# A new step table for the products of a two-layer adaptive-norm and expert kernel: linear products further ahead, copies a step earlier, two operand buffers in turn

## The chip, the cores and the metric

The kernel runs on one core of a Trainium2 chip. The metric is the device time of one execution in microseconds (us), here the median of three runs. The core has five engines that run their own instruction queues and meet only at semaphores: TensorE (PE) multiplies matrices, VectorE (DVE) and ScalarE (ACT) work elementwise, GpSimd (POOL) does one clip and all indirect DMAs, and SyncE (SP) issues most loads and stores. A matmul leaves its result in PSUM, and DVE or ACT must read it before the bank is used again.

## The reference

The input `x` is (4, 1024, 1024). Layer 0 adds a linear product of a gate over a two-way decaying scan; layer 1 adds a mixture of 32 experts (four per token) and a shared network. Cut to what matters:

```
nf, nb = scan(ekv, decay), scan(ekv, decay, reverse=True)       # along time, per channel
df, db = scan(ek, decay),  scan(ek, decay, reverse=True)
out  = sigmoid(r) * (nf + nb - ekv + euk*v) / max(df + db - ek + euk, 1e-8) * (0.8 + 0.2*tf)
x    = x + (out0 @ (weight * scale_weight[:, None]).T + bias)   # r = x, k = v = fside
x    = x + ffn(out1)                                            # out1: same scan, second w and u
ffn(x): h = rmsnorm(x, norm_w); top-4 of softmax(h @ router_w.T)
        routed = sum of topk_w * (silu(h@w1[:, :I]) * (h@w1[:, I:])) @ w2
        shared = (silu(h@sg) * (h@su)) @ sd
        return x + routed + shared
```

All products are made in parts: an operand is split into a high part and a remainder (`hi`, `lo`), and each product is three matmuls for each 128 x 128 block: hi*hi, hi*lo, lo*hi.

## The kernel before

Time runs in three stages.

**Units alone.** The scans are 32 *units*, one for each batch and each 128 channels, on tiles of 128 x 1024. A unit has two passes (`l` = 0 and 1, for the two layers). DVE carries it: four scans and about eight other passes over the tile. ACT supplies exponentials and the inverse, POOL the clip of `k` at 30 (`clip`, L509). The operand of a unit is loaded in two DMAs: `side_t` into the buffer `K`, `x_t` into `X`. There is one `K`, so `load_side(u + 1)` waits until unit u has made its last read of it, in the second pass (`wv_done`, L886). The chain then is the DMA, `clip`, ACT's `side_exp` (L573) and DVE's first operation of the next unit (L867). The first 8 units run with only the splitting of the shared weights beside them.

**Halves.** The tokens are cut into 8 halves of 512. A half is 32 *steps*; a step is one product of 24 matmuls of 512 columns on PE. Steps 0 to 15 mix the linear products of this half (`step_l(o)`, L) with the down products of the half before (`step_d(o)`, D): L0 L1 D0 L2 D1 ... L7 D6 D7. Behind every L product DVE adds it to x (L1192, `XL`, two slots), ACT makes the second gate's sigmoid, DVE multiplies with the ratio (L1185, `C1`) and ACT squares that (L691); PE sums the squares into `SUM_BANK` in `square_sums` (L1339). Behind a D product DVE adds the residual (L1148), PE turns it to token order (`out_by_token`, L1365), ACT copies it to `RS` (`out_copy`, L674) and SP stores it; a copy waits for the store before it. After step 15 comes the *normalization*: DVE and ACT make 1/sqrt of the mean (L1153 to L1161), and PE, DVE and ACT pass the eight normalized tiles through `by_token` (L1349, L1351). Steps 16 to 31 are gate and up products: ACT makes silu, DVE the product (`gated_up`, L1118 and L1124), ACT the high part (L669) and DVE the remainder (L1129). In the last eight of them the next half's operand `C` is loaded (`load_cl`, SP), its high part copied (ACT L726) and its remainder taken (DVE L1139), at the same step.

A product's result lies in one of four PSUM banks, so the product of a step waits until the result of four steps before has been read. Its weights come in two DMAs of 512 KB that SP issues three products ahead.

The units 8 to 31 run inside halves 0 to 5, four in each. The function `fill(h, i, ...)` holds what an engine does at step i, and `unit` calls it at eight fixed places of a unit, so the order of unit work and step work is fixed by the code. Halves 6 and 7 have no units. In half 0 there are no D products.

**Experts.** The routed tokens are 149 tiles of 128 tokens. `step(g, j)` on PE makes four quarter products with the first weights, the transposes of the former tile's activations (L1454) and of the next tile's tokens (L1398), and the second product of the former tile (L1479).

Of the kernel before, what the change touches and what calls it, by code (L numbers as in the profile page):

```python
# [44 lines left out]
def step_d(o):  # L45
    return 2 * o + 2 if o < CB - 1 else 2 * CB - 1
# [10 lines left out]
def adaln_moe(nc, x_t, side_t, cond, w_all, u_all, lin_sb, norm_w, router_t, shared_w, expert_w, out):  # L57
# [12 lines left out]
    with ctx:  # L70
# [85 lines left out]
        lsb_neg = sb("lsb_neg", CB)  # L156

# [30 lines left out]
        xl_sem = [sem(f"xl_in{i}") for i in range(2)]  # L188
# [81 lines left out]
        def with_halves(eng, unit, fill, tail, alone, weights=lambda: None):  # L270


            with eng.Fori(0, 2 * UNITS_PER_HALF - 1) as u:
                unit(u, lambda i: alone(u, i))
            last = 2 * UNITS_PER_HALF - 1

# [6 lines left out]
            unit(last, last_alone)  # L283
            for q in range(UNITS_PER_HALF):
                unit(2 * UNITS_PER_HALF + q, lambda i: fill(0, q * FILLS_PER_UNIT + i, first=True, prev=False, next_=True))
            with eng.Fori(1, HALVES - 2) as h:
                for q in range(UNITS_PER_HALF):
                    unit(h * UNITS_PER_HALF + (2 * UNITS_PER_HALF + q),
# [8 lines left out]
        def _(sp):  # L297
# [47 lines left out]
            def load_xl(h, o):  # L345
                rows, cols = half_rows(h, o)
                wait(sp, "res", h * CB + (o - 1))
                sp.dma_start(XL[o % 2], x_t[rows, cols]).then_inc(xl_sem[o % 2], 16)

            def fill(h, i, first, prev, next_):  # L350
# [3 lines left out]
                if not before_all(h):  # L354
                    for o in range(CB):
                        if i == step_l(o):
                            load_xl(h, o)
                        if i == step_l(o):
                            load_rl(h, o)
                        if prev and i == step_d(o) + 4:  # L360
# [5 lines left out]
                if next_:  # L366
                    for c in range(CB):
                        if i == STEPS - CB + max(c - 1, 0):
# [16 lines left out]
            def unit(u, fill):  # L385
# [25 lines left out]
            def alone(u, i):  # L411

                if isinstance(u, int):
                    return
# [33 lines left out]
        def _(pool):  # L448
# [4 lines left out]
            pool.wait_ge(s["masks"], 4)  # L453
# [6 lines left out]
            pool.wait_ge(s["masks"], 7)  # L460
# [43 lines left out]
            def clip(u):  # L504
# [4 lines left out]
                pool.tensor_scalar(EK, K, 30.0, None, ALU.min).then_inc(s["kc"], 1)  # L509

            clip(0)
            with pool.Fori(1, BLOCKS + 1) as u:
                clip(u)
# [39 lines left out]
        def _(sc):  # L553
# [21 lines left out]
            def load_side(u):  # L575
                wait(sc, "wv_done", 2 * u)
# [982 lines left out]
```

## Time and profile before

| what | value |
|---|---|
| median of three runs | 4997.55 us (4991.03 to 4998.45) |
| the profiled execution, its own time | 4997.07 us |
| its span, first to last instruction | 4995.4 us |
| PE busy | 4492.5 us (90%) |
| DVE busy | 2646.0 us (53%) |
| ACT busy | 1729.7 us (35%) |
| granted TensorE clock, mean | 0.949 of full speed |

The shares are means over three stages with different limits: up to 353 us PE has little to do, to 2298 us PE and DVE share the work, and from there PE is all but full. They have to be read by stage.

### The profile page before, as it was taken

Reading aid. Unit: us, or ns where it says so; the run is one execution under the profiler, and the core shown is the slowest. Engines: PE = TensorE matmul, PEld = TensorE weight load, DVE = VectorE, ACT = ScalarE, POOL = GpSimd, SP = SyncE. Lnnn points to the kernel's source line nnn. Section 1 sums busy time; section 2 is a strip of 40 time slices with the busy share of each in tenths; the row PEclk is TensorE's granted clock in tenths of the full one; section 3 lists DMA queues with packets and bytes.
Section 4 is the critical chain, followed back from the end, with each engine's and each line's share of the span. In section 5 each row is a group of like instructions: output and inputs, shape, how many; then the busy total and the mean of one; then the engine's idle time right before and its main releaser. Section 6 shows DMA issues by size and latency. Waiting matters only on the chain.

```text
span 4995.4 us, 62260 instructions
## 1 busy us (share of the span) xinstructions
PE 4492.5 (90%) x19732; PEld 3555.7 (71%) x19735; DVE 2646.0 (53%) x2844; ACT 1729.7 (35%) x2532; POOL 698.0 (14%) x933
## 2 busy tenths in 40 slices
PE   4446888888888899999999999999999999999998
PEld 1124666666666677877888888788788887888787
DVE  8988878787878774443323343343443235233332
ACT  4444444444444433223223232333432124222331
POOL 1000000000000000541111111111111111111111
PEclk7777999999999999999999999999999999999999
DMA  5564656665656566866435454555654246354442
GB/s 207 206 223 152 222 203 219 206 215 204 218 206 216 201 228 212 238 190 234 109 66 153 110 160 110 156 160 160 210 160 109 59 109 206 78 140 109 142 123 59
DMA packets 247943, 835.17 MB, mean 167 GB/s; under 512 B 28160, under 2 KB 61056, under 8 KB 222976
## 3 DMA queue, kind: packets, MB, share of 16 engines
q1 hardware_dynamic: 172944, 572.77, 32.8%
q0 software_dynamic: 47728, 160.07, 15.0%
q10 hardware_dynamic: 27136, 100.67, 5.4%
q8 instruction: 68, 1.11, 0.1%
q14 instruction: 67, 0.55, 0.0%
HBM read 652.40 MB, written 181.01 MB: 167 GB/s over the span
## 4 chain that ended last, share of the span: by engine, by line
PE 66%; DVE 14%; issue 8%; ACT 6%; DMA 4%; POOL 1%; DVEq 0%; ACTq 0%; SPq 0%; POOLq 0%
PE ps L1465 33%; PE ps L1479 16%; PE ps L1329 10%; PE ps L1398 3%; DMA work<-side_t 2%; DVE work L876 2%; DVE work L873 2%; DVE work L879 1%; POOL work L509 1%; PE ps L1454 1%; DVE work L883 1%; DVE work L886 1%; ACT work L567 1%; ACT work L565 1%; DVE work L900 1%
## 5 line engine op out<-in xcount | busy, mean ns | idle before, releaser
L1465 PE MATMUL ps<-halves 128*128 128x512 f32 x7152 | 1744.3, 396 | 25.4 <-DVE halves L1240 21.8
L1329 PE MATMUL ps<-halves 128*128 128x512 f32 x6144 | 1500.5, 405 | 110.1 <-DVE work L1118 69.5
L1465 PEld LDWEIGHTS ps<-halves 128*128 128x128 f32 x7152 | 1327.7, 189 | 299.2 <-DVE halves L1240 24.0
L1329 PEld LDWEIGHTS ps<-halves 128*128 128x128 f32 x6144 | 1192.0, 195 | 409.1 <-issue 122.4
L1479 PE MATMUL ps<-halves 128*128 128x512 f32 x3576 | 834.9, 389 | 1.3 <-DVE halves L1260 1.3
L1479 PEld LDWEIGHTS ps<-halves 128*128 128x128 f32 x3576 | 671.2, 188 | 140.7 <-DVE halves L1260 1.6
L1244 DVE TENSOR_TENSOR halves<-ps,halves 128x1024 fp32r<-128x1024 f32 x150 | 183.7, 1225 | 927.2 <-ACT halves L757 927.2
L1240 DVE TENSOR_TENSOR halves<-work,halves 128x1024 fp32r<-128x1024 f32 (+1 forms) x320 | 440.5, 1435 | 111.9 <-ACT halves L761 111.9
L757 ACT ACTIVATE halves<-ps 128x1024 fp32r<-128x1024 f32 x150 | 153.8, 1025 | 887.1 <-PE ps L1465 887.1
L761 ACT ACTIVATE halves<-work 128x1024 fp32r<-128x1024 f32 (+1 forms) x320 | 369.7, 1221 | 97.2 <-PE ps L1479 66.5
L509 POOL TENSOR_SCALAR work<-work 128x1024 f32<-128x1024 f32 x33 | 98.0, 2969 | 1728.3 <-DMA work<-side_t 1728.3
L1266 DVE TENSOR_SCALAR work<-ps,acc 128x512 f32<-128x512 f32 x149 | 111.6, 749 | 273.3 <-PE ps L1479 266.6
L1309 PE MATMUL ps<-plain,ident 128*128 128x512 f32 x128 | 88.5, 780 | 184.9 <-ACT halves L641 184.9
L490 POOL DMA_INDIRECT out<-work,add_idx x149 | 236.2, 1585 | 131.0 <-POOL add_idx L487 125.3
L487 POOL COPY add_idx<-acc 128x1 int32 x149 | 27.0, 181 | 1610.2 <-DVE work L1266 1610.2
L1256 DVE TENSOR_TENSOR work<-ps,work 128x256 f32<-128x256 f32 x298 | 124.9, 419 | 231.9 <-ACT work L785 224.1
L795 ACT ACTIVATE work<-ps,acc 128x512 f32<-128x512 f32 x149 | 101.5, 681 | 395.7 <-PE ps L1479 388.5
L1260 DVE TENSOR_TENSOR halves<-ps,halves 128x256 fp32r<-128x256 f32 x298 | 112.2, 419 | 218.6 <-ACT halves L789 218.6
L785 ACT ACTIVATE work<-ps 128x256 f32<-128x256 f32 x298 | 113.3, 380 | 306.0 <-PE ps L1465 305.9
L1309 PEld LDWEIGHTS ps<-plain,ident 128*128 128x128 f32 x128 | 30.0, 250 | 229.0 <-ACT halves L641 197.0
L480 POOL DMA_INDIRECT work<-rows_dram,row_idx x151 | 152.5, 1010 | 129.0 <-POOL row_idx L476 122.8
L789 ACT ACTIVATE halves<-ps 128x256 fp32r<-128x256 f32 x298 | 97.6, 379 | 197.7 <-PE ps L1454 197.7
(179 smaller groups left out, 3893.4 us busy)
## 6 DMA issues: line engine op xcount, KB each, us to landing
halves<-split_dram SPq DMA_DIRECT2D x512, 512.0 KB, 5.1
work<-expert_w SPq DMA_DIRECT2D x192, 1024.0 KB, 5.3
split_dram<-halves ACTq DMA_DIRECT2D x32, 1024.0 KB, 6.0
plain<-shared_w SPq DMA_DIRECT2D x32, 512.0 KB, 4.1
gated_dram<-work ACTq DMA_DIRECT2D x32, 512.0 KB, 3.2
work<-x_t ACTq DMA_DIRECT2D x32, 512.0 KB, 5.2
work<-side_t ACTq DMA_DIRECT2D x32, 512.0 KB, 5.3
ratio_dram<-work ACTq DMA_DIRECT2D x32, 512.0 KB, 3.6
```

The lines of the kernel that those rows point to most:

```text
L480: pool.indirect_dma_start(hx, None, rows_dram[:, :], bass.IndirectOffsetOnAxis(row_idx[:, :].bitcast(u32), 0)).then_inc(s["rows_in"], 16)
L490: pool.indirect_dma_start(out[:, :], bass.IndirectOffsetOnAxis(add_idx[:, :].bitcast(u32), 0), y, None, compute_op=ALU.add).then_inc(s["y_ ...
L509: pool.tensor_scalar(EK, K, 30.0, None, ALU.min).then_inc(s["kc"], 1)
L757: sc.activation(xhi, ps_xt[:, :], ACT.Copy).then_inc(s["x_hi"], 1)
L761: sc.activation(whi[q][:, part], staged(q, part), ACT.Copy).then_inc(s["w_hi"], 1)
L1240: ve.tensor_tensor(wlo[q][:, part], staged(q, part), whi[q][:, part].bitcast(f32), ALU.subtract).then_inc(s["w_lo"], 1)
L1244: ve.tensor_tensor(xlo, ps_xt[:, :], xhi.bitcast(f32), ALU.subtract).then_inc(s["x_lo"], 1)
L1256: ve.tensor_tensor(part, ps_h[:, a * 512 + 256:a * 512 + 512], part, ALU.mult).then_inc(s["act_done"], 1)
L1329: last = pe.matmul(bank(k % 4), w, op[:, part], start=(c == 0 and w is w_hi and op is hi), stop=(c == CB - 1 and w is w_lo))
L1398: last = pe.transpose(ps_xt[:, c * P:(c + 1) * P], hx[:, c * P:(c + 1) * P], ident[:, :])
L1465: last = pe.matmul(ps_h[:, a * 512:a * 512 + 512], xp[:, xk * P:(xk + 1) * P], wp[:, rhs], start=(xk == 0 and xp is xhi and wp is whi[q]), ...
L1479: last = pe.matmul(ps_y[:, h * 512:h * 512 + 512], ap_[:, (q * 2 + k) * P:(q * 2 + k + 1) * P], wp[:, rhs:rhs + 512], start=(q == 0 and k ...
```

## The change

The formulas for the steps become tables. The down products move back, the linear ones forward: L at 0, 1, 2, 4, 6, 8, 10, 11 and D at 3, 5, 7, 9, 12, 13, 14, 15. `XL` has four slots (two of them are the tiles `Z0` and `Z1`, free at that time). The last sum of squares comes after step 14, not 15, and ACT takes the logarithm straight from `SUM_BANK` at step 15 (`R_AT`), ahead of the DVE's own mean; DVE makes `root` and the first two normalized tiles before the last D product's sum. The turns and copies of the outputs have steps of their own. The high part of `C` is copied at steps 23 to 30, its remainder taken at 24 to 31, and its loads are issued from step 22 on.

The two operand buffers are used in turn: in an even unit `side_t` lies in `K` and `x_t` in `X`, in an odd one the other way round. So the next unit's `side_t` is loaded when the first pass has been gated, and `x_t` in the second pass. ACT's `side_exp` moves before the second inverse. In the expert stage PE makes two quarter products before the transposes of the activations, not one.

```diff
+STEP_L = (0, 1, 2, 4, 6, 8, 10, 11)
+STEP_D = (3, 5, 7, 9, 12, 13, 14, 15)
+TURN_AT = (5, 7, 9, 11, 13, 14, 15, 17)
+COPY_AT = (6, 8, 10, 12, 14, 15, 17, 18)
+SQUARE_AT = (3, 4, 5, 7, 9, 11, 13, 13)
+SUM_AT = (5, 5, 6, 8, 10, 12, 13, 14)
+R_AT = 2 * CB - 1
-    return 0 if o == 0 else 2 * o - 1
-    return step_l(o) + 3 if o < CB - 1 else 2 * CB - 1
-    return 2 * o + 2 if o < CB - 1 else 2 * CB - 1
+C_LOAD = (22, 22, 23, 24, 25, 26, 27, 29)
+C_HIGH = (23, 24, 25, 26, 27, 28, 29, 30)
+C_LOW = (24, 25, 26, 27, 28, 29, 30, 31)
...
+        side_of, x_of = (K, X), (X, K)
-        XL, RL, Z, T = [XL0, XL1], [RL0, RL1], [Z0, Z1], SQ
+        XL, RL, Z, T = [Z0, Z1, XL0, XL1], [RL0, RL1], [Z0, Z1], SQ
...
-                        if i == step_l(o):
+                        if i == (step_d(o - 4) + 1 if o >= 4 else o // 2):
                             load_xl(h, o)
-                        if i == step_l(o):
+                        if i == (step_l(o - 2) + 2 if o >= 2 else o):
                             load_rl(h, o)
...
-            def load_side(u):
-                wait(sc, "wv_done", 2 * u)
-                sc.dma_start(K, side_t[ds(u % BLOCKS * P, P), :]).then_inc(s["k_in"], 16)
+            def load_side(u, par):
                 sc.wait_ge(s["gated"], u + 1)
-                sc.dma_start(X, x_t[ds(u % BLOCKS * P, P), :]).then_inc(s["x_in"], 16)
+                sc.dma_start(side_of[par], side_t[ds(u % BLOCKS * P, P), :]).then_inc(s["k_in"], 16)
...
                 fill(5)
+                side_exp(u + 1)
                 fill(6)
                 inverse(1)
                 fill(7)
-                side_exp(u + 1)
...
-                    if i == 2 * CB:
-                        sc.wait_ge(s["mean"], h + 1)
-                        sc.activation(R, SQ, ACT.Ln).then_inc(s["r_ln"], 1)
+                    if i == R_AT:
+                        sc.wait_ge(s["sums"], h * CB + CB)
+                        sc.activation(R, SUM_BANK, ACT.Ln, bias=eps[:, :], scale=1.0 / CH).then_inc(s["r_ln"], 1)
...
+                    if i == 2 * CB:
+                        root(h)
+                        normalize(h, 0)
+                        normalize(h, 1)
...
                 first_product(j, 0)
+                first_product(j, 1)
                 transpose_act(g - 1, 0)
                 transpose_act(g - 1, 1)
-                first_product(j, 1)
                 transpose_x(g + 1)
```

The order on three queues. First PE at the end of the L and D products, in the loop over halves 1 to 5. L1329 (after: L1380) is a product, L1365 (L1416) a turned output, L1339 (L1390) a sum of squares, L1349 and L1351 (L1400, L1402) the first normalized tile. Before:

```order
L1329 MATMUL ps<-halves 128x512 x48
L1362 REGISTER_ALU
L1365 MATMUL ps<-ident,work 128x128 x4
L1339 MATMUL ps<-work,ones 128x512
L200 REGISTER_ALU
L1329 MATMUL ps<-halves 128x512 x24
L1362 REGISTER_ALU
L1365 MATMUL ps<-ident,work 128x128 x4
L1339 MATMUL ps<-work,ones 128x512
L1349 MATMUL ps<-ident,work 128x128 x4
L1351 MATMUL ps<-work,rw 32x512
```

After:

```order
L235 REGISTER_ALU
L1380 MATMUL ps<-halves 128x512 x24
L1413 REGISTER_ALU
L1416 MATMUL ps<-ident,work 128x128 x4
L1390 MATMUL ps<-work,ones 128x512
L235 REGISTER_ALU
L1380 MATMUL ps<-halves 128x512 x24
L1413 REGISTER_ALU
L1416 MATMUL ps<-ident,work 128x128 x4
L1400 MATMUL ps<-ident,work 128x128 x4
L1402 MATMUL ps<-work,rw 32x512
```

The last sum of squares now has a product and a turned output between itself and the first normalized tile; before it stood directly in front of it.

Second, ACT where the third unit of such a half ends and the fourth begins. L726 (after: L771) copies a high part of `C`, L669 (L713) one of the activations, L573 is `side_exp`, L591 (L635) begins the next unit, and the DMA of the ratio closes a unit. Before:

```order
L573 ACTIVATE work<-work 128x1024
L636 DMA ratio_dram<-work 128x1024
L666 REGISTER_ALU
L669 ACTIVATE halves<-work 128x512
L721 ISA
L723 REGISTER_ALU
L726 ACTIVATE halves<-work 128x512
L589 REGISTER_ALU
L591 ISA
L591 ACTIVATE edge_in<-work,edge 128x1
```

After:

```order
L611 ACTIVATE work<-work 128x512
L766 ISA
L768 REGISTER_ALU
L771 ACTIVATE halves<-work 128x512
L680 DMA ratio_dram<-work 128x1024
L710 REGISTER_ALU
L713 ACTIVATE halves<-work 128x512
L771 ACTIVATE halves<-work 128x512
L633 REGISTER_ALU
L635 ISA
L635 ACTIVATE edge_in<-work,edge 128x1
```

Two copies of `C` now stand before the fourth unit's first work where one stood, and `side_exp` has gone from this place.

Third, PE in a tile of the expert stage. L1465 (after: L1516) is a quarter product of 12 matmuls, L1454 (L1505) the transposes of the activations, L1398 (L1449) those of the tokens. Before:

```order
L1465 MATMUL ps<-halves 128x512 x12
L1450 ISA
L200 ISA
L1454 MATMUL ps<-ident,work 128x128 x2
L1450 REGISTER_ALU
L200 REGISTER_ALU
L1454 MATMUL ps<-ident,work 128x128 x2
L1465 MATMUL ps<-halves 128x512 x12
L1395 REGISTER_ALU
L1398 MATMUL ps<-ident,work 128x128 x8
L1465 MATMUL ps<-halves 128x512 x24
```

After:

```order
L1516 MATMUL ps<-halves 128x512 x24
L1501 ISA
L235 ISA
L1505 MATMUL ps<-ident,work 128x128 x2
L1501 REGISTER_ALU
L235 REGISTER_ALU
L1505 MATMUL ps<-ident,work 128x128 x2
L1446 REGISTER_ALU
L1449 MATMUL ps<-ident,work 128x128 x8
L1516 MATMUL ps<-halves 128x512 x24
```

The matmuls are the same; the two groups of transposes have become one.

## Rows read from the trace of the kernel before

**Rows 1.** Busy time by stretch: us, then PE, PEld, DVE, ACT, POOL, PEclk, DMA share, GB/s.

```profile
459.84:1699.84 1240.00, 1059.73 (x4337) 810.16 (x4337) 1006.39 (x906) 525.78 (x774) 59.52 (x20) 0.93 0.61 212
1449.04:1466.09 17.05, 15.41 (x49) 5.18 (x49) 11.55 (x17) 9.01 (x16) 0.00 (x0) 0.83 0.00 1
1466.09:1573.67 107.58, 92.40 (x394) 75.57 (x393) 83.00 (x70) 41.23 (x61) 3.45 (x1) 0.94 0.64 223
1573.67:1699.84 126.17, 105.22 (x429) 81.82 (x429) 106.88 (x97) 54.98 (x79) 8.30 (x3) 0.92 0.67 227
1699.84:1931.21 231.37, 209.15 (x868) 161.70 (x868) 154.97 (x166) 83.47 (x128) 6.21 (x3) 0.94 0.62 214
1824.71:1931.21 106.50, 100.41 (x428) 79.64 (x428) 60.48 (x81) 33.23 (x51) 3.40 (x2) 0.96 0.69 239
```

**Rows 2.** What PE waited for, 1449.04:1699.84: us in total, times, longest.

```profile
PE ps L1349 <- DVE work L1169: 19.7, 2, 10.1
PE ps L1329 <- DVE work L1118: 12.2, 3, 6.8
PE ps L1339 <- ACT work L691: 5.7, 2, 4.2
PE ps L1329 <- DVE halves L1129: 4.1, 1, 4.1
PE ps L1365 <- ACT work L674: 3.7, 1, 3.7
```

**Rows 3.** What DVE waited for in the same period.

```profile
DVE halves L1139 <- ACT halves L726: 14.5, 8, 4.3
DVE work L1124 <- PE ps L1329: 4.7, 1, 4.7
DVE halves L1129 <- ACT halves L669: 3.9, 1, 3.9
DVE work L898 <- issue: 3.5, 5, 1.1
DVE work L867 <- ACT work L573: 2.9, 1, 2.9
DVE work L1157 <- ACT work L701: 2.9, 1, 2.9
DVE work L898 <- ACT work L614: 1.4, 1, 1.4
```

**Rows 4.** What DVE waited for in the stretch 0:459.84.

```profile
DVE work L867 <- ACT work L573: 15.2, 8, 2.8
DVE plain L1185 <- ACT work L569: 4.3, 4, 1.1
```

**Rows 5.** Timeline, PE in half 6 and ACT in half 4: start, us, line, count.

```profile
2004.05 54.73 PE L1329 MATMUL ps<-halves 128*128 128x512 f32 x240
...
1488.24 0.60 ACT L674 ACTIVATE work<-ps 128x512 f32<-128x512 f32 x1 [10.99 <-DMA out<-work]
```

**Rows 6.** Landing of SP's weight loads, 1466:1600: count, KB, median us.

```profile
halves<-split_dram SPq DMA_DIRECT2D x38, 512.0 KB, 4.6
```

**Rows 7.** Timeline of POOL and DVE where a clip runs beside DVE.

```profile
1575.53 0.69 DVE L1139 TENSOR_TENSOR halves<-work,halves 128x512 fp32r<-128x512 f32 x1 [1.22 <-ACT halves L726]
...
1579.45 2.77 POOL L509 TENSOR_SCALAR work<-work 128x1024 f32<-128x1024 f32 x1 [59.21 <-DMA work<-side_t]
1579.99 1.05 DVE L1139 TENSOR_TENSOR halves<-work,halves 128x512 fp32r<-128x512 f32 x1 [2.03 <-ACT halves L726]
```

**Rows 8.** Timeline of PE in one tile of the expert stage.

```profile
3008.36 2.89 PE L1465 MATMUL ps<-halves 128*128 128x512 f32 x12
3011.09 0.60 PE L1454 MATMUL ps<-ident,work 128*128 128x128 f32 x4
3011.44 3.02 PE L1465 MATMUL ps<-halves 128*128 128x512 f32 x12
3014.30 1.04 PE L1398 MATMUL ps<-ident,work 128*128 128x128 f32 x8
```

More of the change, by code:

```diff
@@ L187, in adaln_moe @@
         put_sem = [sem(f"put_out{i}") for i in range(PUTS)]
-        xl_sem = [sem(f"xl_in{i}") for i in range(2)]
+        xl_sem = [sem(f"xl_in{i}") for i in range(4)]
         w_in = [sem(f"w_in{q}") for q in range(GROUPS)]
@@ L270, in with_halves @@
         def with_halves(eng, unit, fill, tail, alone, weights=lambda: None):
-            with eng.Fori(0, 2 * UNITS_PER_HALF - 1) as u:
-                unit(u, lambda i: alone(u, i))
+            with eng.Fori(0, UNITS_PER_HALF - 1) as v:
+                for par in range(2):
+                    unit(2 * v + par, par, lambda i: alone(2 * v + par, i))
             last = 2 * UNITS_PER_HALF - 1
+            unit(last - 1, 0, lambda i: alone(last - 1, i))
             def last_alone(i):
@@ L281, in last_alone @@
                     weights()
-            unit(last, last_alone)
+            unit(last, 1, last_alone)
             for q in range(UNITS_PER_HALF):
-                unit(2 * UNITS_PER_HALF + q, lambda i: fill(0, q * FILLS_PER_UNIT + i, first=True, prev=False, next_=True))
+                unit(2 * UNITS_PER_HALF + q, q % 2, lambda i: fill(0, q * FILLS_PER_UNIT + i, first=True, prev=False, next_=True))
             with eng.Fori(1, HALVES - 2) as h:
                 for q in range(UNITS_PER_HALF):
-                    unit(h * UNITS_PER_HALF + (2 * UNITS_PER_HALF + q),
+                    unit(h * UNITS_PER_HALF + (2 * UNITS_PER_HALF + q), q % 2,
                          lambda i: fill(h, q * FILLS_PER_UNIT + i, first=False, prev=True, next_=True))
@@ L346, in load_xl @@
                 rows, cols = half_rows(h, o)
-                wait(sp, "res", h * CB + (o - 1))
-                sp.dma_start(XL[o % 2], x_t[rows, cols]).then_inc(xl_sem[o % 2], 16)
+                if o < 2:
+                    wait(sp, "l_tr", h)
+                else:
+                    wait(sp, "res", h * CB + (o - 3))
+                sp.dma_start(XL[o % 4], x_t[rows, cols]).then_inc(xl_sem[o % 4], 16)
             def fill(h, i, first, prev, next_):
@@ L383, in store_out, with unit @@
                 sp.dma_start(to, RS.rearrange("p (t c) -> p t c", c=P)).then_inc(s["o_out"], 16)
-            def unit(u, fill):
+            def unit(u, par, fill):
                 for i in range(FILLS_PER_UNIT):
@@ L508, in clip @@
                 apart(pool)
[L509 to L513, printed above, removed]
+                pool.tensor_scalar(EK, side_of[par], 30.0, None, ALU.min).then_inc(s["kc"], 1)
+            clip(0, 0)
+            with pool.Fori(0, BLOCKS // 2) as v:
+                clip(2 * v + 1, 1)
+                clip(2 * v + 2, 0)
             pool.wait_ge(s["zero_set"], 1)
@@ L1199, in fill @@
                             ve.wait_ge(s["c1"], h * CB + (o + 1))
-                            ve.scalar_tensor_tensor(RES[:, part], XL[o % 2], lsb[:, CB + o:CB + o + 1], C1[o],
+                            ve.scalar_tensor_tensor(RES[:, part], XL[o % 4], lsb[:, CB + o:CB + o + 1], C1[o],
                                                     ALU.add, ALU.add).then_inc(s["res"], 1)
                     if i == 2 * CB:
-                        normalize(h)
+                        for o in range(2, CB):
+                            normalize(h, o)
+                        split_z_lo(h, CB - 1)
                     if i == 2 * CB + 2:
@@ L1411, in half @@
                     for o in range(CB):
-                        if i == square_step(o):
+                        if i == sum_step(o):
                             square_sums(h, o)
-                        if not first and i == step_d(o) + (2 if o < CB - 2 else 1):
+                        if not first and i == turn_step(o):
                             out_by_token(h - 1, o)
```

95 lines of the change are left out of this document (56 added, 39 removed).

## The prediction, made before the changed kernel ran

> **What bounds the kernel now.** I read the time by stretch first [rows 1]. A *period* goes from one half's first normalized tile to the next half's. Five periods with units in them, from 459.84 to 1699.84, take 1240.0 us, so 248.0 each. In one of them the normalized tiles take 17.05 us, the sixteen gate and up products 107.58, and the sixteen L and D products with the normalization behind them 126.17. Neither engine is full: over the five periods PE is busy 1059.7 us of 1240.0 and DVE 1006.4. The two wait for each other through the four banks.
>
> Then I read who waits. PE [rows 2] waits for the first normalized tile (19.7 us in two places, 10.1 in the larger), for DVE to free a bank (12.2), for a square (5.7), for the remainder of the activations that D0 reads (4.1), and for an output copy (3.7). DVE [rows 3] waits 14.5 us for the high parts of C, because ACT makes them in the same step, 4.7 for a late up product, 3.9 for a high part that stands on ACT behind an output copy, 2.9 for `side_exp` and 2.9 for the root.
>
> DVE is the engine to count with. It has 83.00 us of work in the gate stage and 106.88 in the L and D stage [rows 1]. PE's own time is less: ten products take 54.7 us in half 6, where nothing holds them [rows 5], so sixteen take 88; and a whole L and D stage without units takes 106.5, of which PE is busy 100.4 and idle 6.1, nearly all of it before the first normalized tile [rows 1].
>
> **The gate stage (108 us, six times).** The tables take three waits of DVE away or shorten them. The high part of C comes a step before its remainder, so the 11 to 14.5 us go: I count 11 here and the rest in the L and D stage, since two of the eight stand behind the stage's end. The 4.7 us for the up product went with PE's 3.7 us wait for the output copy, which moves behind the next product. Of the 3.9 us on the high part some 3.5 stays: ACT waits for the store of output 6 before it copies output 7 (10.99 us idle before that copy [rows 5]), and the store is still issued at step 18. The 1.4 and one 1.1 of L898 stay (ACT's inverse stands behind that copy), and about 1.1 us of short gaps between the two operations of `gated_up`. So DVE needs 83.0 + 3.5 + 1.5 + 1.1 + 1.1 = 90.2 us, against a PE floor of 88. Set beside each other step by step (5.5 us a product on PE; on DVE, per fill, 6.7 us for three scans, 5.5 for the next four operations, 1.2 and 3.9 or 5.1 for the rest), the bank for step 30 is free at 75 and wanted at 78, and the one for the next half's step 0 is free at 90.2 and wanted at 89.5. Both waits for banks (12.2 us) shrink to under 1. **The stage goes from 107.6 to 90.2.**
>
> **The L and D stage (126 us, five times with units).** D0 now follows three L products, so the 4.1 us wait for the remainder goes. The linear result has two steps until its gate is multiplied in all places but two, so most of the short waits on L1185 and L898 go; `side_exp` is early (2.9). The root: ACT's logarithm starts at the last sum, which comes one product (5.5 us) sooner. DVE's wait of 2.9 goes, and 1.3 us of DVE work (the last residual) moves behind the first normalized tile, where DVE waits anyway. So DVE needs 106.9 - 1.3 + 2.6 (waits that stay) = 108.2 us, against PE's 100.4. PE will still stand: in the step-by-step table at the turns of outputs 0, 1, 4 (1.5, 1.6 and 2.4 us, DVE's sum comes late), at the sums 1, 2 and 4 (0.9, 0.7, 1.8) and before the first normalized tile (3.7 us, down from 10.1). **The stage goes from 126.2 (mean of five some 124.8) to 108.2.**
>
> A period is then 17.05 + 90.2 + 108.2 = 215.4 us. Five periods: 1240.0 - 5 x 215.4 = 163 us saved.
>
> **Half 5's gate stage and halves 6 and 7.** From 1699.84 to 1931.21 it was 231.4 us. I expect 17.05 + 90.2 + 105.7 = 213, so 18.4 saved. Without units DVE is no bound. The root there is hidden less than it looks: at step 15 ACT first copies output 5, which waits for the store of output 4, issued when product 14 is done. That store lands 5 to 6 us later, about at the end of product 15, and only then comes the logarithm. So of 6.1 us idle some 4.3 stay, and sum 1 must wait 0.9 for its square, which waits for sum 0 in the same step. Net 0.8 each; one is in the 18.4, the other adds 0.8.
>
> **The units alone and the first half.** L867 waited 15.2 us for `side_exp` in eight places [rows 4]. All go: the side load is issued some 9 us earlier. Of L1185's 4.3 us three of four go (3.2), with 3.6 us of L898 and the root. That is 15.2 + 3.2 + 3.6 = 22. What stays: the C copies of the last lone unit keep their steps, and I take nothing for them.
>
> **The clip** runs beside other DVE work now. A DVE operation beside it took 1.05 us instead of 0.69 [rows 7]. That was paid before too, so I count zero; the bounds are -0.4 and +0.4 for each of 32, 12 us either way. No row shows a clip beside a scan, which it may now meet.
>
> **The rule that speaks against this.** The Trainium skill, "SBUF — State Buffer", section "Who interferes with whom", says that the port pair which VectorE shares with GpSimd is held for a whole instruction and the other engine blocks fully. By it a DVE operation with two SBUF inputs behind a clip would stand up to 2.8 us, and at 32 clips some 2.1 us more than I count the sum would be 67 us higher. The row does not agree: L1139 has two SBUF inputs, began 0.5 us into the clip and lost 0.36.
>
> **The expert stage.** In a tile the quarter product before the transposes takes 2.73 us to the next start (3008.36 to 3011.09), the same one after them 2.86 (3011.44 to 3014.30) [rows 8]. One of two changes between products and transposes goes, so 0.13 us in each of 147 tiles: 19 us. The transposes come 2.9 us later; the second product that needs them starts 9.5 us behind them now (3.2 to the tokens' transposes, 0.8 for those, 5.5 for two quarter products) and 6.6 then. Between stand two ACT and two DVE operations of 256 columns each, so I see no new wait. Bounds: 0, and +1 us a tile (147) if the splits came late.
>
> **What takes some of it back.** SP is one queue. Before, a load of C at step 23 + c stood ahead of the weights for step 27 + c and waited for the remainder of c - 2; now the same wait stands at step 21 + c, ahead of the weights of step 25 + c. By the table the weights of step 29 are asked for at 66.4 (DVE's remainder of C2) and land 4.6 to 6 us later [rows 6], at 71 to 72.5; PE wants them at 72.8. There is no slack. I add 3 us to each of the six halves with units: 18.
>
> **The sum.** 163 + 18.4 + 0.8 + 22 + 19 - 18 = 205 us. The profiled execution took 4997.1, its span 4995.4, the median 4997.55: they agree, so 4997.1 - 205 = **4792 us**.
>
> **The rivals.**
> *A: DVE's order holds.* PE's waits come back elsewhere, and only the waits that DVE itself loses count: 14.5 + 2.9 + 2.9 a period [rows 3], 101 in five, 12 in the sixth, 22 at the start, 19 in the experts, 154 together, less 8 for SP: 4851. For it: DVE meets its step work only at eight fixed places of a unit. Against: in the table those places fit.
> *B: no queue bites.* Without the 18 us, and with a period near DVE's busy time (201.3, and the 5.5 us of the 17.05 in which DVE is not busy [rows 1], 207) instead of 215.4: 43 more, 4731.
> *C: the tables do not do what they say.* The blocked ACT queue (a square waits for the former sum, an output copy for a store) takes as much from DVE as the C copies gave, and only the 22 us at the start, half of A's 101 and 5 us in the experts come: 4920.
> *D: slower than before.* Place: SP between steps 23 and 29. If DVE runs later than in my table, the weights for steps 28 to 31 come late one after another, PE makes the products late, and DVE gets them late. It decides when the remainder of C2 is later than 67 on the table's clock; if each of the eight products from step 24 stands 5 us for its weights, six halves lose 240 us where the sum without its 18 gained 223: 5014. Against it: PE's longest waits in these stages are all for DVE or ACT, none for weights [rows 2].
> *E: the lock rule,* DVE stands behind the clip: 4792 + 67 = 4859.
>
> **How the numbers follow.** Forecast 0.62 (4765 to 4825), A 0.18, B 0.07, C 0.06, E 0.03, D 0.04. To hold eight in ten the range takes the forecast's own, A's 4851 with some room, and part of B's: 4745 to 4870. A measurement of this kernel tells about 0.2% (10 us) from no change: faster 0.94, same 0.02, slower 0.04.
>
> **What would show it.** In the profile after: the five periods at 215 us (right) or 228 and more (A); DVE's wait for the high parts of C under 2 us a period; PE's wait for the first normalized tile 3 to 5 us, not 10; no wait of PE for banks above 1 us; eight waits of L867 gone; an expert tile at 17.6 us, not 17.7. I would be wrong if PE waits for weights (its own issue) at steps 27 to 31, if ACT's idle time before edges or copies grows, or if the second product of a tile waits for L1260.

## The result

The changed kernel took 4811.9 us (median of four runs, 4806.2 to 4814.7), the kernel before 4998.0 (four runs): ratio 0.963, 95% interval 0.9618 to 0.9641. The forecast was 4792 with a range of 4745 to 4870: the direction and the range hold, and the gain is 186 us where I had 205. The profiled execution took 4814.7 us, its span 4813.0.

By stretch, from the first normalized tile of one half to that of the next (where before begins its stretches is in [rows 1]), in us:

| stretch | before | after | gain forecast | gain measured |
|---|---|---|---|---|
| start, lone units and half 0 | 459.84 | 437.28 | 22 | 22.6 |
| five periods | 1240.0 | 1111.75 | 163, less 15 for SP | 128.3 |
| half 5's gates, half 6 | 231.37 | 209.23 | 18.4, less 3 for SP | 22.1 |
| to half 7 | 208.64 | 206.51 | 0.8 | 2.1 |
| half 7's end | 158.75 | 158.52 | 0 | 0.2 |
| experts | 2696.8 | 2689.7 | 19 | 7.1 |

The busy time of the changed kernel, by stretch, with the columns of [rows 1]; the second and third lines are the normalized tiles with the gate stage, and the L and D stage, of the period that [rows 2, 3] are from:

```profile
437.28:1549.03 1111.75, 1029.65 (x4336) 787.66 (x4336) 1009.39 (x905) 526.54 (x774) 69.67 (x20) 0.97 0.66 236
1322.50:1430.05 107.55, 102.89 (x441) 77.75 (x441) 96.30 (x88) 51.89 (x79) 6.61 (x2) 0.98 0.62 217
1430.05:1549.03 118.98, 102.94 (x428) 79.79 (x428) 105.68 (x95) 53.61 (x77) 6.58 (x2) 0.95 0.69 246
1549.03:1758.26 209.23, 201.87 (x868) 155.69 (x868) 155.41 (x166) 83.37 (x128) 7.28 (x3) 0.99 0.68 237
```

The first line says that the work of DVE is what it was (1009.4 us for 1006.4) in 128 us less. PE's busy time fell by 30.1 us and its mean granted clock rose from 0.93 to 0.97 of full speed; no run separates what the clock gave from what the shorter waits gave. The second line comes to the forecast's 17.05 + 90.2 within 0.3 us. The third does not: 119.0 against 108.2. What PE waited for there, and then DVE, over the whole period (us in total, times, longest):

```profile
PE ps L1380 <- DVE work L1163: 9.3, 2, 6.7
PE ps L1416 <- DVE work L1193: 4.9, 3, 1.9
PE ps L1400 <- DVE work L1215: 3.3, 1, 3.3
...
DVE work L1163 <- issue: 9.4, 1, 9.4
DVE work L1215 <- PE ps L1402: 2.9, 6, 0.5
DVE work L943 <- issue: 2.6, 4, 1.1
DVE halves L1174 <- ACT halves L713: 2.4, 1, 2.4
DVE work L1169 <- DVE work L1163: 1.9, 8, 0.5
```

Set against [rows 2, 3] the waits that the tables aimed at are gone: no wait for the high parts of C (14.5), 3.3 us before the first normalized tile instead of 10.1 in the longer of two places, none for D0's remainder, 0.6 for an output copy instead of 3.7. But there is a new one, the longest: DVE stands 9.4 us in front of L1163, `gated_up` of the half's last block, and what ended the wait is nothing that the profile shows ("issue"). PE then waits 6.7 us for the bank. In the five periods this happens in four places (DVE timeline: start, us, line, idle before):

```profile
770.25 0.69 DVE L1163 TENSOR_TENSOR work<-ps,work 128x512 f32<-128x512 f32 x1 [4.58 <-issue]
998.95 0.69 DVE L1163 TENSOR_TENSOR work<-ps,work 128x512 f32<-128x512 f32 x1 [9.64 <-issue]
1220.16 0.69 DVE L1163 TENSOR_TENSOR work<-ps,work 128x512 f32<-128x512 f32 x1 [4.21 <-issue]
1447.21 0.69 DVE L1163 TENSOR_TENSOR work<-ps,work 128x512 f32<-128x512 f32 x1 [9.39 <-issue]
```

In those waits DMA was busy as follows (columns of [rows 1]; the last but one is the share):

```profile
765.70:770.20 4.50, 4.50 (x22) 3.72 (x21) 0.00 (x0) 0.00 (x0) 0.00 (x0) 1.00 0.37 140
989.30:999.00 9.70, 4.85 (x22) 3.69 (x20) 0.06 (x2) 0.00 (x0) 0.00 (x0) 0.97 1.01 390
1216.00:1220.20 4.20, 3.37 (x15) 2.44 (x13) 0.04 (x1) 0.00 (x0) 0.00 (x0) 1.00 0.36 138
1437.80:1447.20 9.40, 3.44 (x16) 2.51 (x14) 0.02 (x1) 0.00 (x0) 0.00 (x0) 0.91 0.96 371
```

Two things stand out. The four places are exactly those where the loop over halves 1 to 5 jumps back on DVE; from half 0 to half 1, where there is no jump, L1163 follows without a gap, and that period is the shortest (213.4 us; the others 222.2, 228.0, 221.7 and 226.5). And the wait is 4.2 to 4.6 us where the DMA engines are a third busy and 9.4 to 9.6 where they are full. The kernel before has the same wait in the same four places, before its L1118, but only 9.9 us of it in all:

```profile
838.28 0.69 DVE L1118 TENSOR_TENSOR work<-ps,work 128x512 f32<-128x512 f32 x1 [1.94 <-issue]
1089.17 0.69 DVE L1118 TENSOR_TENSOR work<-ps,work 128x512 f32<-128x512 f32 x1 [3.44 <-issue]
1337.39 0.69 DVE L1118 TENSOR_TENSOR work<-ps,work 128x512 f32<-128x512 f32 x1 [2.00 <-issue]
1587.32 0.69 DVE L1118 TENSOR_TENSOR work<-ps,work 128x512 f32<-128x512 f32 x1 [2.57 <-issue]
```

### The profile page after: what moved, and what is told of

Its sections match the earlier page's. It is cut to its first block, busy times and chain, and to the rows that moved or that the text cites. A ratio compares the mean times of both kernels' runs of the same rounds, so it can differ in the third digit from the quotient of the medians.

```text
span 4813.0 us, 62132 instructions
## 1 busy us (share of the span) xinstructions
PE 4442.4 (92%) x19732; PEld 3532.2 (73%) x19735; DVE 2640.3 (55%) x2844; ACT 1717.7 (36%) x2532; POOL 719.2 (15%) x934
## 4 chain that ended last, share of the span: by engine, by line
PE 68%; DVE 17%; issue 8%; ACT 4%; DMA 2%; DVEq 0%; ACTq 0%; SPq 0%; POOL 0%; POOLq 0%
PE ps L1516 34%; PE ps L1530 17%; PE ps L1380 11%; PE ps L1449 3%; DVE work L924 2%; DVE work L918 2%; DVE work L945 1%; DVE work L943 1%; PE ps L1505 1%; DVE work L934 1%; DVE work L928 1%; DMA out<-work 1%; DVE work L921 1%; PE ps L1402 1%; DVE work L931 1%
## 5 line engine op out<-in xcount | busy, mean ns | idle before, releaser
L1516 PE MATMUL ps<-halves 128*128 128x512 f32 x7152 | 1701.4, 394 | 25.5 <-DVE halves L1291 22.0
L1516 PEld LDWEIGHTS ps<-halves 128*128 128x128 f32 x7152 | 1340.4, 189 | 303.6 <-DVE halves L1291 24.1
L1380 PE MATMUL ps<-halves 128*128 128x512 f32 x6144 | 1466.6, 398 | 47.1 <-DVE work L1163 25.4
L1380 PEld LDWEIGHTS ps<-halves 128*128 128x128 f32 x6144 | 1162.3, 190 | 329.8 <-issue 71.1
L1530 PE MATMUL ps<-halves 128*128 128x512 f32 x3576 | 834.9, 389 | 1.3 <-DVE halves L1311 1.3
L550 POOL TENSOR_SCALAR work<-work 128x1024 f32<-128x1024 f32 x33 | 118.3, 3585 | 1524.4 <-DMA work<-side_t 1524.4
L528 POOL COPY add_idx<-acc 128x1 int32 x149 | 27.3, 183 | 1606.7 <-DVE work L1317 1606.7
L924 DVE TENSOR_TENSOR_SCAN work<-decay,edge_in,work 128x1024 f32<-128x1024 f32 x64 | 156.2, 2440 | 1.0 <-ACT edge_in L635 1.0
L1449 PE MATMUL ps<-ident,work 128*128 128x128 f32 x1200 | 155.5, 273 | 0.0
```

The lines of the kernel that those rows point to most:

```text
L924: ve.tensor_tensor_scan(F[:, ::-1], d, F[:, ::-1], edge_in[:, 0:1], ALU.mult, ALU.add).then_inc(s["h_bwd"], 1)
L1380: last = pe.matmul(bank(k % 4), w, op[:, part], start=(c == 0 and w is w_hi and op is hi), stop=(c == CB - 1 and w is w_lo))
L1449: last = pe.transpose(ps_xt[:, c * P:(c + 1) * P], hx[:, c * P:(c + 1) * P], ident[:, :])
L1516: last = pe.matmul(ps_h[:, a * 512:a * 512 + 512], xp[:, xk * P:(xk + 1) * P], wp[:, rhs], start=(xk == 0 and xp is xhi and wp is whi[q]), ...
L1530: last = pe.matmul(ps_y[:, h * 512:h * 512 + 512], ap_[:, (q * 2 + k) * P:(q * 2 + k + 1) * P], wp[:, rhs:rhs + 512], start=(q == 0 and k ...
```

## The experiments

The theory: after the jump DVE has to fetch its code again, through the same DMA engines as the data. The first rival was that the wait is for something late in any case. Nine of the runs ran on chips (14, 12 and 9 of the record) on which both kernels took some 130 us longer, at one place (last section). The other three (`after_old_tables`, `after_late_exp`, `before_early_c`) ran on a chip without it, where the kernel before took 4997.0 us. So the ratios of changed kernels from the nine are compared with that of `after_same`, 0.9638 (0.9622 to 0.9654), the changed kernel unaltered; the others with the 4811.9 us of the result:

> The changed kernel itself, unaltered, so that the other runs can be set beside it. Expected: the ratio to the kernel before that was measured at first, 0.963, or slightly above where this chip adds the same time to both; the four waits in front of L1163 again near 4.6, 9.6, 4.2 and 9.4 us.

There its four waits are 4.0, 9.4, 4.1 and 9.7 us, and its five periods 1110.3 us.

**The loop written out.** `after_straight`:

```diff
-            with eng.Fori(1, HALVES - 2) as h:
+            for h in range(1, HALVES - 2):      # VectorE alone
                 for q in range(UNITS_PER_HALF):
```

> The changed kernel, with VectorE's loop over halves 1 to 5 written out as straight code; the other engines keep theirs. In the changed kernel DVE stands 4.6, 9.6, 4.2 and 9.4 us (27.8 in all) in front of L1163 at exactly the four places where this loop jumps back, released by nothing that the profile shows, and half 0 to half 1, where there is no jump, has no such wait. Theory J (the jump makes DVE fetch its code again): the four waits go, and as DVE sets the pace of these halves the time falls by 20 to 28 us, to 4784 to 4792. Rival K (the wait is for something that comes late anyway, or straight code has to be fetched as well and stalls as long elsewhere): less than 5 us, 4807 to 4815.

Ratio 0.956 (0.9546 to 0.9575) against 0.9638: 39 us by ratio, but that is across two chips. The two traces side by side, the long place left out, differ by 30 us: 33.5 less in the five periods, 3.3 less in the stretch behind them, 6.8 more from half 7 to the end. In the five periods no wait for "issue" above 1.1 us is left on DVE, and the periods are 213.6, 215.5, 216.5, 215.4 and 215.8. Its windows for the same two stages:

```profile
1298.40:1404.31 105.91, 102.50 (x440) 77.56 (x441) 96.37 (x88) 51.87 (x79) 6.00 (x2) 0.98 0.63 222
1404.31:1514.24 109.93, 99.09 (x429) 77.44 (x429) 105.77 (x95) 53.23 (x77) 6.42 (x2) 1.00 0.75 266
```

The L and D stage falls from 119.0 to 109.9. The five periods gain more than the four waits (27.2 us in `after_same`). In the loop a register computation stands between the two operations of `gated_up` (register instructions of DVE's sequencer, whose trace rows lie between L1163 and L1169); written out, the gap L1169 <- L1163 falls from 8.7 us in the five periods to 0.7. Theory J holds, rival K falls.

`before_straight` is the same edit of the kernel before.

> The kernel before, with the same loop written out. There the four waits in front of L1118 are 1.9, 3.4, 2.0 and 2.6 us, 9.9 in all, and DVE is less often the one that is waited for. Theory J: 4 to 10 us less than the kernel before. If the jump costs nothing here, then the change made it costly by taking away what hid it: 0 to 3 us. Rival K: no difference.

Ratio 0.9973 (0.9963 to 0.9984), 14 us, somewhat above the expected 4 to 10. So the jump was not free before either. The list of this kernel also has a wait marked "issue" once in a half, 3.3 to 5.8 us in five places, such as

```profile
1466.36 0.69 DVE L1130 TENSOR_TENSOR work<-ps,work 128x512 f32<-128x512 f32 x1 [4.90 <-issue]
```

It is not a new one. L1130 here is L1124 in the kernel before, the operation that waits for the late up product [rows 3]. In all five places it starts 0.1 us after PE's last matmul of that product ends, and in the five periods the two kernels' lists have the same wait under two names (kernel before, then this one):

```profile
DVE work L1124 <- PE ps L1329: 20.8, 6, 5.7
...
DVE work L1130 <- issue: 18.7, 4, 5.7
```

"Issue" says only that the profile found no releaser; here it was PE. Such a name has to be checked against the other engines' rows. The waits in front of L1163 pass that check: in the one that ends at 1447.21 PE and ACT stand still as well, PE until 1447.96 and ACT until 1448.84, both for DVE.

**Where the loop lies.** Why 28 us now and 10 before? Three edits move DVE's code and leave its order and its transfers alone, by waits at its start on a semaphore that is soon set. The waits take time themselves: DVE's first operation starts at 8.8, 11.2 and 14.9 us instead of 6.5.

```diff
             ve.wait_ge(s["cond_in"], 32)
+            # 24, 48 or 81 more instructions (two such waits each)
```

> The changed kernel with 24 more instructions at the very start of VectorE's program (waits on a semaphore that is set by then), so that all that follows stands 24 instructions later in its code. The packets of the instruction queue q14 carry 0.47 MB / 57 = 8.2 KB, 128 instructions of 64 bytes. In the compiled program the body of the loop over halves begins at instruction 396 in the kernel before (place 12 in a block of 128) and at 477 in the changed one (place 93, 35 left); here it is 501 (place 117, 11 left). Theory P (the wait after the jump depends on where the body begins in such a block, since a second block is needed soon): the four waits stay as long as in the changed kernel or grow, 28 us or more in all. Theory T (only the traffic that the change puts at the start of a half, x for four blocks at once, makes them long): the four waits stay as they are, 4 to 5 and 9 to 10. So this one tells little alone; it stands beside the next.

> The same with 48 more instructions: the body of the loop begins at 525 (place 13 of 128, as in the kernel before). Theory P: the four waits fall to those of the kernel before, 2 to 3.5 us each, 10 us in all instead of 28, and the time falls by 12 to 18 us. Theory T: nothing changes, 28 us in all and the same time within 3 us.

The four waits, from the DVE timelines of `after_pad24` and of `after_pad48`:

```profile
768.36 0.69 DVE L1164 TENSOR_TENSOR work<-ps,work 128x512 f32<-128x512 f32 x1 [1.75 <-issue]
990.29 0.69 DVE L1164 TENSOR_TENSOR work<-ps,work 128x512 f32<-128x512 f32 x1 [5.00 <-issue]
1208.64 0.69 DVE L1164 TENSOR_TENSOR work<-ps,work 128x512 f32<-128x512 f32 x1 [1.82 <-issue]
1429.23 0.69 DVE L1164 TENSOR_TENSOR work<-ps,work 128x512 f32<-128x512 f32 x1 [4.56 <-issue]
...
770.86 0.69 DVE L1164 TENSOR_TENSOR work<-ps,work 128x512 f32<-128x512 f32 x1 [1.77 <-issue]
995.00 0.69 DVE L1164 TENSOR_TENSOR work<-ps,work 128x512 f32<-128x512 f32 x1 [4.90 <-issue]
1215.04 0.69 DVE L1164 TENSOR_TENSOR work<-ps,work 128x512 f32<-128x512 f32 x1 [2.03 <-issue]
1436.35 0.69 DVE L1164 TENSOR_TENSOR work<-ps,work 128x512 f32<-128x512 f32 x1 [2.98 <-issue]
```

13.1 and 11.7 us instead of 27; the times are 15.6 and 10.1 us below `after_same` (ratios 0.9608, 0.9592 to 0.9624, and 0.9617, 0.9601 to 0.9633), the five periods 1092.4 and 1097.0, 17.9 and 13.4 less. Theory P had looked for 12 to 18 us from `after_pad48`; of what is missing 3.3 us are the padding's own time at the start. Theory T (traffic alone) falls: nothing but the place changed. My rule for the place falls as well: I had expected `after_pad24`, with 11 instructions left in its block, to stay at 28. `before_pad81` does the reverse to the kernel before.

> The kernel before with 81 more instructions at the start of VectorE's program, which puts the body of its loop over halves at instruction 477, place 93 of 128, where the changed kernel has it (there the four waits are 28 us, and 12 and 13 us with it at places 13 and 117). Its own traffic and order are untouched. If the place of the code alone makes the waits long: 4 to 5 us and 7 to 10 us in front of L1118 in turn, 23 to 28 in all instead of 10, and 5 to 15 us slower than before. If it takes the transfers and the order of the changed kernel as well: the four stay at 2 to 3.5, and the time within 3 us of before.

It gave 4.2, 7.5, 4.1 and 6.1 us (21.8 in all, for 9.9), and 1.0036 (1.0021 to 1.0050), 19 us slower. Some 8 of these are the padding's own time at the start (DVE's first operation at 14.95 instead of 6.54 us); the five periods take 15.9 us more. So the place of the code alone makes most of the difference: with the loop at 477 both kernels wait 4 us in two places and 6 to 10 in the other two, at 396, 501 and 525 about 2 and 2.6 to 5. (The numbers are places in the compiled program; no trace shows them.)

The rows of DVE's sequencer show what the place adds. L323 is the loop: COMPARE_BRANCH is the jump back, FUSED_REGOPS the first instruction behind it. These are the fourth jumps of the changed kernel (`gated_up` then starts at 1447.21) and of `after_pad24` (at 1429.23), with count, duration in ns and start in us:

```profile
L323 DVEq COMPARE_BRANCH  x1: 63/63/63, 1436.6 to 1436.6; - x1
L323 DVEq FUSED_REGOPS  x1: 74/74/74, 1442.2 to 1442.2; - x1
...
L323 DVEq COMPARE_BRANCH  x1: 63/63/63, 1423.5 to 1423.5; - x1
L323 DVEq FUSED_REGOPS  x1: 74/74/74, 1429.1 to 1429.1; - x1
```

The first instruction comes some 5.5 us after the jump in both. Behind it `gated_up` follows in 0.1 us in `after_pad24`, but in 5.0 us in the changed kernel: there is a second wait. This holds in every jump of every kernel here that keeps the loop. From the jump to the first instruction it is 2.7 to 3.3 us in the first and third jump and 3.5 to 6.0 in the second and fourth, wherever the loop lies. From there to `gated_up` it is 0.1 us with the loop at 396, 501 and 525, and with it at 477, in both kernels, 2.3 to 2.6 and 3.4 to 5.1. At the loop's end, where the same branch is not taken, the next instruction comes after 0.1 us. So the place decides whether a second wait follows the first. That it is a second block of code is argued from the instruction queue: q14 brings four packets in 989.30:999.00 of the changed kernel and two in 985.2:990.3 of `after_pad24`. Which places have it is open: three without and one with do not give a rule.

The long waits go with full DMA engines: in the four of `before_pad81` the DMA share is 0.35, 0.89, 0.36 and 0.95. `before_early_c` (below) leaves DVE's code where it is and moves transfers: its four waits are 1.75, 3.96, 1.72 and 4.74 us at shares of 0.07, 1.04, 0.05 and 1.03, where the kernel before has 1.94, 3.44, 2.00 and 2.57 at 0.52, 0.84, 0.53 and 0.99. Nearly idle DMA engines do not take the short waits below 1.7 us. Long and short waits alternate by half in every kernel, and no run took the traffic out of a long one, so that traffic is what lengthens them is likely but not shown.

**ScalarE's loop too.** `after_straight_two` writes out the loop on both engines.

> The changed kernel with the loop over halves 1 to 5 written out on VectorE and on ScalarE. On VectorE alone this gave a ratio of 0.956 and periods of 215.4 us (222 to 228 in the changed kernel). What was left there: ACT's high part at L713 waits 8.6 us for nothing that the profile shows, at ScalarE's own jump, and DVE then 2.8 us for ACT at L1174. Theory J for ScalarE too: these 2.8 us go in most of four places, and 1 to 2 us of short gaps a half, 5 to 15 us faster than with VectorE's alone. If ScalarE's jump is hidden behind its idle time: within 4 us of that.

Ratio 0.9565 (0.9549 to 0.9581), the same as with VectorE alone within the intervals; the five periods take 1073.1 us for 1076.8. The sizes say 4 to 6 us at most. These two are the fastest kernels of the study, 0.8% below the changed one.

**The parts of the change.** One by one, taken out of the changed kernel or put into the one before.

```diff
-C_LOAD = (22, 22, 23, 24, 25, 26, 27, 29)
-C_HIGH = (23, 24, 25, 26, 27, 28, 29, 30)
+C_LOAD = (24, 24, 25, 26, 27, 28, 29, 30)
+C_HIGH = (24, 25, 26, 27, 28, 29, 30, 31)
```

> The changed kernel, with the loads of C and their high parts in halves 0 to 5 put back to the steps of before (loads at 24, 24, 25 to 30, high parts at 24 to 31, in the same step as their remainders). The prediction counted 11 us of DVE's wait in each gate stage for this and 3 us against it for SP. If that is right, 8 to 14 us in each of six halves come back: 4860 to 4896. If DVE's order held anyway and the wait had been hidden behind PE: under 20 us, 4812 to 4832.

Ratio 0.9795 (0.9780 to 0.9810) against 0.9638: 80 us by ratio, inside what the first theory expected. By stage, in the four periods with a jump and against `after_same`, it costs 11.8 us in the gate stage and 1.6 in the L and D stage. The wait is back as it was:

```profile
DVE halves L1184 <- ACT halves L771: 13.7, 8, 4.3
```

The same tables put into the kernel before, and nothing else:

> The kernel before, with the loads of C a step or two earlier and the high parts a step ahead of their remainders, as in the changed kernel, and nothing else. Taking these out of the changed kernel cost 80 to 88 us (ratio 0.9795 against 0.9638). If the parts add up: 65 to 88 us less than before, ratio 0.983 to 0.987. If in the kernel before PE's own waits (the output copy ahead of the late up product, 3.7 and 4.7 us) take most of it: 20 to 50 us less, ratio 0.990 to 0.996.

Ratio 0.9836 (0.9820 to 0.9853), 82 us. The part is worth the same alone and with the others: it adds up, and it is the largest one that was measured.

```diff
-STEP_L = (0, 1, 2, 4, 6, 8, 10, 11)
-STEP_D = (3, 5, 7, 9, 12, 13, 14, 15)
+STEP_L = (0, 1, 3, 5, 7, 9, 11, 13)
+STEP_D = (2, 4, 6, 8, 10, 12, 14, 15)
...
```

> The changed kernel with the steps of the sixteen L and D products, of the squares and their sums, of the turns and the output copies put back to those of before (L and D in turn, D0 at step 2, the last square and its sum at step 15); x keeps its four slots, C, the side loads, the early logarithm and the expert tiles stay changed. The prediction took the L and D stage from 124.8 us (mean) to 108.2, by D0 behind three L products, two steps of room for each gate, and the last sum a product sooner. If the tables carry this: 8 to 16 us in each of six halves come back, 50 to 95 us above the changed kernel, and halves 6 and 7 lose 1 to 3 us each. If what gave it was x in four slots and the early `side_exp`: under 20 us.

Ratio 0.9740 (0.9723 to 0.9756), 55 us above the changed kernel; the start loses 6.3 us, the first period 3.2, the four others 7.6 to 9.3 each, the stretch to half 6 6.9, the one to half 7 1.3. The total is at the low end of what was expected, but it falls in another stage: in the four periods with a jump the gate stage takes 6.5 us more on average and the L and D stage only 2.2. The expectation looked for all of it in the L and D stage. The waits there are those of [rows 2, 3]: with the old steps PE stands 3.7 us for an output copy and DVE 5.7 us for the up product behind it, and in the changed kernel neither does.

```diff
-                side_exp(u + 1)
                 fill(6)
                 inverse(1)
                 fill(7)
+                side_exp(u + 1)
```

> The changed kernel with one line moved: `side_exp` of the next unit stands behind fill 7 again, as in the kernel before. The buffers in turn, and so the early side load, stay. The prediction counted for the early step 2.9 us a period and, together with the early load, 15.2 us in eight lone units. If its place matters: L912 waits again in each unit, 1.5 to 3 us for each of 32, 30 to 60 us in all, less what other waits hide. If the early load alone was enough: under 8 us.

Ratio 0.9631 (0.9614 to 0.9647), 4812.3 us: no difference. With the early load in place, moving `side_exp` adds nothing; no run took the early load out.

```diff
                 first_product(j, 0)
+                first_product(j, 1)
                 transpose_act(g - 1, 0)
                 transpose_act(g - 1, 1)
-                first_product(j, 1)
```

> The kernel before, with nothing changed but the order in an expert tile: the second quarter product stands ahead of the transposes of the activations. The prediction priced this at 19 us (0.13 in each of 147 tiles). In the changed kernel the whole expert part is 7.1 us shorter. If the price of this edit is what the trace now shows: 5 to 9 us less than before. If the full 19 were there and lost to something else in the changed kernel: 15 to 20.

Ratio 0.9986 (0.9976 to 0.9995), 7 us. From tile to tile (median) it is 17.73 us before, 17.69 here and 17.68 in the changed kernel. 82, 55, 7 and the 22.6 of the start are 167 of 186 us; six of the start's are also in the tables' 55, so some 25 us are left to what no run took apart: the early side load in the periods, x in four slots and the early logarithm.

## Why the prediction held, and where it did not

**The gate stage** (107.6 to 90.2): right, 90.5 in the period shown, and for the reasons given. Its 11 us for C measured 11.8 (`after_old_c`). Its other large term, the late up product behind an output copy (4.7), is most of the 6.5 that `after_old_tables` loses there.

**The L and D stage** (to 108.2): the size is right without the jump (109.9), wrong with it (119.0, and 114.3 in the halves where the wait is 4 us). The account is only in part shown. The forecast took 16.6 us off this stage, by D0's place, the room for the gates, `side_exp` and the earlier root. The new places of the products are worth 2.2 there and those of C 1.6; moving `side_exp` is worth nothing. What the side load, the four slots and the early logarithm gave was not taken apart. One detail came out: PE's waits at the turns of outputs were put at 5.5 us a period, and are 27.3 in five. Written out, the five periods are 1076.8 us, 163.2 below [rows 1], where the sum had 163. That is nearer than its terms deserve: the gate stage is then 1.3 us better than the forecast and the L and D stage 1.7 worse, and the forecast had not counted on losing the register gaps.

**The 18 us for SP's queue**: wrong. PE waited for weights 2.1 us in four places over the five periods, so this cost did not exist, and rival D, which was built on it, had no ground. It was luck that it stood in the sum: it took the place of part of the jump's cost, 27.8 us where [rows 1] held 9.9. Even so the five periods gained 20 us less than the sum had, and the experts 12 less. What the prediction missed is that it took a wait by "issue" for a constant. L1118's wait stood in the trace of before, in four places, and I neither priced it nor asked what its size hangs on.

**Rival A** (4851, periods of 228 and more): two periods came near it (228.0, 226.5), but for the jump; without it all are under 217, so waits that come back elsewhere in DVE's order did not show. **B**'s period (207) was never reached. **C** fell: `after_old_c` and `after_old_tables` show that both tables gain, 80 and 55 us.

**The start**: right (22.6 for 22), though `after_late_exp` shows that the place of `side_exp` did nothing; the load is what is left. **The clip at zero**: right in sum, DVE's busy time in the five periods is 1009.4 for 1006.4. A clip itself got longer; from the page, its mean and then the mean of the same line before (2969 ns):

```profile
L550 POOL TENSOR_SCALAR work<-work 128x1024 f32<-128x1024 f32 x33 | 118.3, 3585 | 1524.4 <-DMA work<-side_t 1524.4
```

The 20 us fell on POOL. ACT waited for its clip 27.6 us in the whole execution, and 167.5 before. So the lock rule of **rival E** (the Trainium skill, "SBUF — State Buffer", "Who interferes with whom") did not show again: beside 20 clips in the five periods DVE was busy 3 us longer than before, where 2.1 us each would be 42.

**The experts** (19): the size was off, 7.1. The price of a change between products and transposes, 0.13 us, was read from one tile, and the tile as a whole was not checked against it. In the changed kernel one tile reads at the same place (PE timeline):

```profile
2990.62 5.61 PE L1516 MATMUL ps<-halves 128*128 128x512 f32 x24
2996.06 0.60 PE L1505 MATMUL ps<-ident,work 128*128 128x128 f32 x4
2996.50 1.04 PE L1449 MATMUL ps<-ident,work 128*128 128x128 f32 x8
2997.29 5.74 PE L1516 MATMUL ps<-halves 128*128 128x512 f32 x24
```

From the transposes to the next start it is 0.44 us now, 0.35 in [rows 8]: of 0.13 saved, 0.09 is given back. The 0.04 left fits the medians (17.73 to 17.69 and 17.68), and 0.04 to 0.05 a tile over 147 tiles is the 7 us.

**Halves 6 and 7**: 0.8 each was low; the tables alone are worth 1.3 in half 7 and the whole change 2.1.

The other signs that the prediction named: PE's wait for the first normalized tile (3 to 5) is 3.3; DVE's for the high parts of C is zero. Of the eight waits for `side_exp` in the start seven are gone; the first unit's stays (3.9). An expert tile is 17.68, not 17.6. "No wait for banks above 1 us" failed, with 6.7 us, by the jump. One sign of being wrong did come: ACT's idle time before output copies grew, in the five periods from 46.1 us to 111.8. It cost nothing, since PE waits only 2.5 us there for such a copy, where it was 14.8.

## What to carry to other kernels

When an edit takes the slack out of an engine's program, every stall that the slack covered comes to the top; list the waits marked "issue" before predicting, above all at the back edge of a loop, and ask what their size depends on. A stall of that kind can be moved by writing the loop out, or by shifting the code, and it changes with any edit that adds instructions, so a small gain or loss of a kernel with such a loop may be the place of its code: here 10 to 19 us of 5000. But "issue" only means that no releaser was found; look first whether another engine ended something at that moment. A step table set up from measured durations was good to 2 us in 108 for a stage as a whole, and put the gain of its own edits in the wrong stage; taking the parts out one by one, and reading the runs by stage, is what showed it.

## What the runs showed of the hardware

The idle time of DVE at a jump back was 1.7 to 5.0 us in three placings of the code and 4.0 to 9.7 us in the one that two kernels shared, and in the changed kernel more than twice as long with the DMA engines full as with them a third busy. What comes in then, from the DMA view of the changed kernel at 1437:1448 (packets, MB, share):

```profile
q14 instruction: 5, 0.04, 1.0%
```

Over the whole span q14 had 70 packets in the changed kernel, 57 with VectorE's loop written out and 44 with both loops. The Trainium skill, "Runtime: NRT & Kernel Launch", section "Instruction fetch mechanics", says that a taken branch to code outside the small window an engine holds must wait for a DMA fetch, and that straight code is fetched ahead and mostly hidden. The runs agree with both: the waits stand behind the taken jumps (3 to 6 us to the next instruction, 0.1 where the branch is not taken) and go with them, and with the loop written out no wait above 1.1 us without a releaser is left on DVE in the five periods of `after_straight`.

In the nine runs with the long place the stretch from half 6 to half 7 took 332 to 338 us in every kernel, instead of 206 to 209. It is the stretch in which POOL issues 106 of its 128 indirect DMAs of `slots_dram`; in `before_swap` DVE stands 61 us for the transfer of x and 63 us at an output sum, and for most of that time the DMA engines move 1 GB/s (DVE timeline, then the DMA view of 2040:2190 in 40 slices):

```profile
2116.85 0.75 DVE L1192 SCALAR_TENSOR_TENSOR work<-ps,lsb,work 128x512 f32<-128x512 f32 x1 [60.84 <-remote]
...
2182.06 0.69 DVE L1148 TENSOR_TENSOR work<-ps,work 128x512 f32<-128x512 f32 x1 [62.88 <-remote]
...
GB/s 200 113 1 126 156 1 1 1 1 1 1 46 95 1 1 1 1 1 1 1 42 101 1 1 1 1 1 1 1 58 83 1 1 1 1 1 0 0 206 73
...
slots_dram<-acc POOLq DMA_INDIRECT x106
```

In the runs of the other chips the same transfers hold up nothing. It weighs on both sides of each ratio alike (337.6 us in `before_swap`, 333.2 in `after_same`), and its cause is open.
